# A decoder's last cross-attention on Trainium2: the keys' weights folded into the queries' weights, computed on the chip

## What is computed

```
x = x + attn(ln(x))                  layer 0, 16 heads, softmax
x = x + xattn(ln(x), ctx)            layer 0, 16 heads, softmax
x = x + ffn(ln(x))                   layer 0, int4 weights and a low-rank part
x = x + attn(ln(x))                  layer 1, 16 heads, rotary, sigmoid
x = x + xattn1(ln(x), ctx)           layer 1, one head: the change is here
x = x + experts(ln(x))               layer 1, two of 64 matrices per chunk of 128 rows

xattn1:  query = z @ Wq + bq;  key = ctx @ Wk + bk;  value = ctx @ Wv + bv
         weights = softmax(query @ key.T * 256 ** -0.5);  weights @ value
```

## Time and profile before

| | |
|---|---|
| median of 3 runs | 1092.56 us (1092.5 to 1093.98) |
| the profiled execution: its own time, its span | 1093.21 us, 1091.3 us |
| TensorE busy, matmuls / weight loads | 1026.3 us (94%) / 802.1 us (74%) |
| VectorE, ScalarE, GpSimd busy | 758.2, 637.0, 578.8 us |
| TensorE in the chain that ended last | 81% of the span |

### The profile page before, as it was taken

The page is one execution under the profiler, slowest core; times in us unless marked ns, Lnnn a source line. Parts: engine busy times, 40 slices in busy tenths (PEclk is TensorE's granted clock), DMA queues, the critical chain, the costliest instruction groups (busy, mean ns, idle before and its releaser), DMA issues.

```text
span 1091.3 us, 24379 instructions
## 1 busy us (share of the span) xinstructions
PE 1026.3 (94%) x8490; PEld 802.1 (74%) x8490; DVE 758.2 (69%) x1748; ACT 637.0 (58%) x1160; POOL 578.8 (53%) x924
## 2 busy tenths in 40 slices
PE   5689999999999999999999999999999999999976
PEld 4456777777766777777777778787878766888854
DVE  4577778788776656666677887777877643587772
ACT  2335666566566676666654566676767777555430
POOL 3343453554445545555557898787787720124340
PEclk9889999999999999999999999999999999999989
DMA  6976677656646445654453446767575892036556
GB/s 200 120 101 89 109 98 90 97 85 87 87 64 88 70 74 93 117 93 92 92 81 46 60 58 92 84 88 88 75 95 70 102 107 31 15 98 186 149 160 212
DMA packets 123626, 104.94 MB, mean 96 GB/s; under 512 B 26841, under 2 KB 123241, under 8 KB 123497
## 3 DMA queue, kind: packets, MB, share of 16 engines
q1 hardware_dynamic: 117794, 99.71, 56.9%
q10 hardware_dynamic: 5712, 3.68, 1.6%
HBM read 29.47 MB, written 4.19 MB: 31 GB/s over the span
## 4 chain that ended last, share of the span: by engine, by line
PE 81%; DVE 6%; DMA 4%; issue 3%; SPq 2%; ACT 2%; POOL 1%; ACTq 1%; POOLq 0%; DVEq 0%
PE l_sT L1096 11%; PE l_ring L1181 11%; PE l_o L1116 11%; PE l_copy L1162 8%; PE l_ring L1131 7%; PE l_ring L1218 7%; PE l_copy L1139 4%; PE l_ring L1201 4%; DVE l_nmax L948 3%; PE l_copy L1116 3%; PE l_ring L1229 3%; PE l_sT L1760 2%; DMA qstack<-l_qpart 2%; PE l_ring L1831 2%; SPq L506 2%
## 5 line engine op out<-in xcount | busy, mean ns | idle before, releaser
L948 DVE TENSOR_REDUCE l_nmax<-l_ring 128x2 f32<-128x512 f32 (+1 forms) x384 | 250.1, 676 | 105.3 <-PE l_ring L1131 99.7
L747 ACT ACTIVATE l_probs<-l_sT 128x1024 f32<-128x1024 f32 (+1 forms) x256 | 256.7, 1023 | 68.3 <-PE l_sT L1096 55.9
L1096 PE MATMUL l_sT<-qstack,kstack 99*128 99x256 bf16 (+2 forms) x1280 | 186.1, 272 | 0.5 <-ACT l_probs L747 0.5
L1131 PE MATMUL l_ring<-kstack,qstack 96*128 96x256 bf16 (+1 forms) x1024 | 140.1, 249 | 19.2 <-DVE l_nmax L948 6.1
L1096 PEld LDWEIGHTS l_sT<-qstack,kstack 99*128 99x128 bf16 (+2 forms) x1280 | 126.7, 104 | 20.8 <-issue 1.6
L1131 PEld LDWEIGHTS l_ring<-kstack,qstack 96*128 96x128 bf16 x1024 | 75.6, 98 | 75.7 <-DVE l_nmax L948 23.2
L1116 PE MATMUL l_o<-l_probs,v_heads 128*32 128x256 f32 (+1 forms) x2048 | 127.4, 383 | 0.0
L1181 PE MATMUL l_ring<-wT,l_zT 128*128 128x256 f32 x512 | 124.5, 381 | 1.0 <-DVE l_nmax L948 0.8
L606 POOL TENSOR_SCALAR factors<-mv 128x2 f32<-128x2 f32 (+1 forms) x77 | 21.7, 282 | 166.6 <-DVE mv L1005 140.5
L1162 PE MATMUL l_copy<-l_zT,wT 128*128 128x256 f32 x384 | 101.3, 396 | 3.6 <-ACT l_q L794 1.8
L1181 PEld LDWEIGHTS l_ring<-wT,l_zT 128*128 128x128 f32 x512 | 91.7, 190 | 13.5 <-issue 2.8
(11 more groups left out here) (207 smaller groups left out, 1972.6 us busy)
## 6 DMA issues: line engine op xcount, KB each, us to landing
qstack<-l_qpart SPq DMA_DIRECT2D x288, 128.0 KB, 4.4
kstack<-l_kpart SPq DMA_DIRECT2D x192, 128.0 KB, 5.6
kstack<-in_experts SPq DMA_DIRECT2D x36, 256.0 KB, 3.1
kstack<-l_kpart SPq DMA_DIRECT2D x96, 60.0 KB, 3.3
qstack<-in_experts SPq DMA_DIRECT2D x20, 256.0 KB, 3.1
out_y<-x_res SPq DMA_DIRECT2D x16, 256.0 KB, 3.7
l_cx<-in_ctx SPq DMA_DIRECT2D x32, 90.0 KB, 2.9
x_res<-in_x SPq DMA_DIRECT2D x1, 2048.0 KB, 15.8
```

What stands on the lines that cost most here:

```text
L747: act.activation(probs[buffer_of(g)][0:kp, :], sT[g % 2][0:kp, :], ACT.Sigmoid if sig(u) else ACT.Exp, scale=HD ** -0.5).then_inc(p_ok, 1)
L948: dve.tensor_reduce(nmax[u % 2][:, tt, h0:h0 + hb], bank("s", u, i)[:, 0:hb * sk].rearrange("p (h k) -> p h k", h=hb), AX_X, ALU.max, nega ...
L1096: i = pe.matmul(sT[g % 2][0:kp, j * S:(j + 1) * S], kstack[slot_of(u)][0:rows_used, col * width(u) + kt * kp:col * width(u) + (kt + 1) * k ...
L1131: m = pe.matmul(out[:, j * sk:(j + 1) * sk], qstack[slot_of(u)][0:STACK, (h0 + j) * S + tt * P:(h0 + j) * S + (tt + 1) * P], kstack[slot_o ...
```

## The change

Before, queries and keys are projected apart. After, scores are (z M + m) times the context itself: M is the queries' weights times the keys' weights transposed, m the queries' bias times the same. The context gets a column of ones, by which the keys' bias joins the product, so the context rows are 194 wide with a column of zeros. The values' bias is a row of the values' weights and meets the same column of ones. In detail:

- Four new jobs on the layers' copy bank, one each in periods 35 to 38, all behind `qT`: `ma` transposes the queries' weights, `mb` the keys' weights, `mc` multiplies them, `md` multiplies the queries' bias. TensorE fills the bank, ScalarE empties it; GpSimd clears the folded keys' buffer in `ma`.
- The jobs `k` leave TensorE and ScalarE, from DRAIN twice and from TAIL_ORDER. `s` reads the transposed context, of which three buffers are used instead of two.
- The eviction of the values goes from VectorE (an add of the bias) to ScalarE (a copy).
- In `t.w`, the values' bias is one row instead of a broadcast over 128 partitions, GpSimd clears one block of 128 partitions instead of two of 64, and SyncE waits for that before its last two loads.
- VectorE sets the ones and zeros columns of the context's two buffers once.

```diff
-        rows st e3 p1k vb rope_k fz sT4 p2q pa fxb e4 z e5 fst dk2 sT5 pb qT sT6 fa e6 ffac sT7 p2k kT dq1 xb e7 fac fb""",
+        rows st e3 p1k vb rope_k fz sT4 p2q pa fxb e4 z e5 fst dk2 sT5 pb qT ma mb mc md sT6 fa e6 ffac sT7 p2k kT dq1
+        xb e7 fac fb""",
...
-        "qB": (15,), "t.w": (20,)}
+        "qB": (15,), "t.w": (20,), "ma": (35,), "mb": (36,), "mc": (37,), "md": (38,)}
...
-TAIL_ORDER = "cl fac s q hash choose z y rows2 v pT rows k out mean add z2 cx"
+TAIL_ORDER = "cl fac s q hash choose z y rows2 v pT rows out mean add z2 cx"
...
+            def fold_pads():
+                pool.wait_ge(copy_full, copied["ma", 0, 0] + 1)
+                pool.memset(fold_k, 0.0).then_inc(fold_zeros, 1)
...
+            def folded_weights(job):
+
+                copy_out(job, 0)
+                halves = copy_bank[:, :].rearrange("p (k f) -> p k f", k=KT)
+                if job == "ma":
+                    act.wait_ge(ring_full, ring["pb", B - 1, 0] + 1)
+                    i = act.activation(fold_q, halves, ACT.Identity)
+                elif job == "mb":
+                    act.wait_ge(fold_zeros, 1)
+                    act.activation(fold_k[:, :, 0:P], halves[:, :, 0:P], ACT.Identity)
+                    act.activation(fold_k[:, :, P + LAST_C:2 * P - 2], halves[:, :, P:C], ACT.Identity)
+                    i = act.activation(fold_k[:, :, 2 * P - 2:2 * P - 1], t["col_c_bk"][:, :].unsqueeze(2), ACT.Identity)
+                elif job == "mc":
+                    i = act.activation(folded, halves, ACT.Identity)
+                else:
+                    i = act.activation(fold_col[:, :], copy_bank[:, 0:KT], ACT.Identity)
+                i.then_inc(copy_empty, 1)
...
+            def fold(job):
+                out = copy_slot(job, 0)
+                halves = out[:, :].rearrange("p (k f) -> p k f", k=KT)
+                if job in ("ma", "mb"):
+                    tail_weights_there(pe)
+                    for k in range(KT):
+                        for e in range(KT):
+                            i = pe.transpose(halves[:, k, e * P:(e + 1) * P], (raw_q if job == "ma" else raw_k)[:, e, k * P:(k + 1) * P],
+                                             ident[:, :])
+                elif job == "mc":
+                    pe.wait_ge(copy_empty, copied["mb", 0, 0] + 1)
+                    for e in range(KT):
+                        for k in range(KT):
+                            i = pe.matmul(halves[:, e, :], fold_q[:, k, e * P:(e + 1) * P], fold_k[:, k, :],
+                                          start=(k == 0), stop=(k == KT - 1))
+                else:
+                    pe.wait_ge(late_dma, LATE_DMAS)
+                    for e in range(KT):
+                        for k in range(KT):
+                            i = pe.matmul(out[:, e:e + 1], fold_k[:, k, e * P:(e + 1) * P], t["col_c_bq"][:, k:k + 1],
+                                          start=(k == 0), stop=(k == KT - 1))
+                i.then_inc(copy_full, 1)
...
-            for name in ("c_wq", "c_wk", "c_wv"):
+            for name in ("c_wq", "c_wk"):
                 sp.dma_start(w[name][:, 0, :], d[name][0:P, :]).then_inc(w_dma, 16)
                 rest = d[name].shape[0] - P
-                sp.dma_start(w[name][P - rest:P, 1, :], d[name][P:P + rest, :]).then_inc(w_dma, 16)
-            sp.dma_start(bc_v[:, :], d["c_bv"].rearrange("(a n) -> a n", a=1).broadcast_to((P, D))).then_inc(w_dma, 16)
+                sp.dma_start(w[name][0:rest, 1, :], d[name][P:P + rest, :]).then_inc(w_dma, 16)
+            sp.dma_start(w["c_wv"][:, 0, :], d["c_wv"][0:P, :]).then_inc(w_dma, 16)
+            sp.wait_ge(pads_ok, 1)
+            sp.dma_start(w["c_wv"][LAST_C:P - 2, 1, :], d["c_wv"][P:C, :]).then_inc(w_dma, 16)
+            sp.dma_start(w["c_wv"][P - 2:P - 1, 1, :], d["c_bv"].rearrange("(a n) -> a n", a=1)).then_inc(w_dma, 16)
...
-            for name in ("c_wk", "c_wv"):
-                pool.memset(w[name][0:2 * P - C, 1, :], 0.0).then_inc(pads_ok, 1)
+            pool.memset(w["c_wv"][:, 1, :], 0.0).then_inc(pads_ok, 1)
...
-        def keys(b):
-            act.wait_ge(ctx_ps, ctx_no("k", b) + 1)
-            if b < 2:
+        def values(b):
+            act.wait_ge(v_ps, v_no("v", b) + 1)
+            if b == 0:
                 wait(act, m["parts_free"])
...
+            if b > 1:
+                act.wait_ge(out_ps, b - 1)
+            act.activation(v[b % 2][:, :], v_bank[0:SC, 0:D], ACT.Identity).then_inc(v_out, 1)
...
-                    i = pe.matmul(s_bank[:, tt * SC:(tt + 1) * SC], qT[b % 2][:, k, tt * P:(tt + 1) * P], kT[b % 2][:, k, :],
+                    i = pe.matmul(s_bank[:, tt * SC:(tt + 1) * SC], qT[b % 2][:, k, tt * P:(tt + 1) * P], cxT[b % 3][:, k, :],
```

More of the change, by code:

```diff
@@ L211, in jobs_of @@
     return out
-TAIL_ORDER = "cl fac s q hash choose z y rows2 v pT rows k out mean add z2 cx"
-TAIL_LEAD = {"s": 0, "pT": 0, "out": 0, "q": 1, "k": 1, "v": 1, "z": 2, "rows": 3, "cx": 2, "cl": 3, "fac": -1, "add": -5, "y": -6}
+TAIL_ORDER = "cl fac s q hash choose z y rows2 v pT rows out mean add z2 cx"
+TAIL_LEAD = {"s": 0, "pT": 0, "out": 0, "q": 1, "v": 1, "z": 2, "rows": 3, "cx": 2, "cl": 3, "fac": -1, "add": -5, "y": -6}
 def tail_jobs(p):
@@ L285, in layers_stage @@
                 copies_before[u], last_outputs = len(copied), u
-            opens = job in ("z", "fz", "cx", "nT", "aT", "qT", "kT", "w", "qA") or job in ("qa", "ka") and kind_of(u) != "sigmoid"
+            opens = job in ("z", "fz", "cx", "nT", "aT", "qT", "kT", "w", "qA", "ma", "mb", "mc", "md") or job in ("qa", "ka") and kind_of(u) != "sigmoid"
             if opens:
@@ L313, in layers_stage @@
         attnT = sb("attnT", [P, KT, S], F32)
-        cx = [sb(f"cx{i}", [SC, C], F32) for i in range(2)]
+        cx = [sb(f"cx{i}", [SC, C + 2], F32) for i in range(2)]
         cxT = [sb(f"cxT{i}", [P, 2, SC], F32) for i in range(3)]
@@ L376, in layers_stage @@
             "ring_free": [(ring_empty, len(ring))]})
[L377 to L382, removed]
+        tail_weights_there = tail["weights_there"]
         def w_loads(eng, j, dst, done):
@@ L721, in _ @@
                         quantised(i)
+                    elif job == "ma":
+                        fold_pads()
                     elif job == "np":
@@ L847, in _ @@
                         lora_rows()
+                    elif job in ("ma", "mb", "mc", "md"):
+                        folded_weights(job)
                     elif job == "e":
@@ L1285, in _ @@
                         transposed_weight(u, raw[u % 4], copy_slot("w", u)).then_inc(copy_full, 1)
+                    elif job in ("ma", "mb", "mc", "md"):
+                        fold(job)
                     elif job == "qA":
@@ L1338, in tail_programs @@
     first_bank = [job for job in jobs if job[0] in ("z", "z2")]
-    second_bank = [job for job in jobs if job[0] in ("k", "cx")]
+    second_bank = [job for job in jobs if job[0] == "cx"]
     third_bank = [job for job in jobs if job[0] in ("v", "hash")]
@@ L1507, in queries @@
                 wait(act, m["whole_free"]["qk"[b]])
+                wait(act, m["fold_there"])
             else:
@@ L1557, in do @@
                 queries(b)
-            elif job == "k":
-                keys(b)
+            elif job == "v":
+                values(b)
             elif job == "cx":
@@ L1612, in rows2 @@
             normalise(z2, b).then_inc(rows2_ok, 1)
[L1614 to L1622, removed]
         def residual(b):
@@ L1679, in bits @@
                 dve.memset(work[:, 0, b:b + 1], float(2 ** b))
-                i = dve.memset(work[:, 1, b:b + 1], float(2 ** b - 2 ** NB))
-            link(i)
+                dve.memset(work[:, 1, b:b + 1], float(2 ** b - 2 ** NB))
+            wait(dve, m["cx_free"])
+            for buf in cx:
+                dve.memset(buf[:, C:C + 1], 1.0)
+                i = dve.memset(buf[:, C + 1:C + 2], 0.0)
+            i.then_inc(ones_ok, 1)
+            dve.wait_ge(ones_ok, 1)
         def do(job, b):
@@ L1759, in queries @@
                 for k in range(KT):
-                    i = pe.matmul(q_bank[:, j * S:(j + 1) * S], w["c_wq"][:, k, j * P:(j + 1) * P], zT[b % 2][:, k, :],
+                    i = pe.matmul(q_bank[:, j * S:(j + 1) * S], folded[:, k, j * P:(j + 1) * P], zT[b % 2][:, k, :],
                                   start=(k == 0), stop=(k == KT - 1))
             i.then_inc(q_ps, 1)
-        def keys(b):
-            weights_there(b)
-            pe.wait_ge(ctx_out, ctx_no("k", b))
-            for j in range(KT):
-                for k in range(KT):
-                    i = pe.matmul(ctx_bank[:, j * SC:(j + 1) * SC], w["c_wk"][:, k, j * P:(j + 1) * P], cxT[b % 2][:, k, :],
-                                  start=(k == 0), stop=(k == 1))
-            i.then_inc(ctx_ps, 1)
         def values(b):
-            weights_there(b)
-            pe.wait_ge(ctx_out, ctx_no("cx", b) + 1)
+            pe.wait_ge(ctx_out, b + 1)
             if b > 0:
```

(2 more changed lines are left out.)

63 lines of the change are left out of this document (33 added, 30 removed), and 14 rows, old and new, of the table DRAIN.

## The result

| | before | after |
|---|---|---|
| median of the runs | 1093.27 us (1092.5 to 1094.37) | 1105.07 us (1101.85 to 1108.33) |
| profiled execution, its span | 1093.21, 1091.3 us | 1106.16, 1104.3 us |
| granted clock over the span | 0.989 | 0.983 |

A forecast was written before the change was run, and what follows sets the result against it. TensorE was taken to bound the layers' sigmoid periods and the tail. Folds +7.2, SyncE's wait in period 20 +2.4 and tail -0.8 gave +8.8 us, 1101.4 us for the median, range 1097.2 to 1104.6.

The forecast's parts named there:

- The folds: Four sigmoid periods of the layers: waits plus work of ma, mb, mc, md cost +7.2 us (6.5 to 8.5).
- 0.93 for each wait: Behind the queries' transposes, TensorE waits 0.93 us per fold until ScalarE has emptied the shared PSUM bank.
- Rival 2: Layers: the four fold waits are absorbed, 3.7 of 7.2 us vanish, total +5.1, 1097.7 us; chance 10%.
- The tail: Removed keys jobs gain nothing in middle periods, as output waits for ScalarE's evictions; tail sum -0.8 us (-4.1 to +0.6).
- a bound (0.17): Tail's middle periods: if ScalarE overlapped both evictions, the output would start at 1003.33, gaining 0.17 us a period.
- about 0.5 was forecast for that far: Tail's start: removed keys job takes 0.89 off the first output, values' eviction adds 0.38 to the second; 0.5 left.
- t.w: Period 20: SyncE's wait for GpSimd's clearing delays the stack copies, so TensorE starts 2.4 us later (0 to 3.4).
- the same 4.2 to land: Period 20: after the twelfth stack copy at 469.47, an unchanged 4.2 us landing lets TensorE start at 473.7.
- rival 4: At 471.3 the long TensorE wait halves the clock, costing 2.5 us more: +11.3, 1103.9 us; chance 10%.
- a row of 2 us without work: Kernel's end, 1054 to 1056: clock stayed at 1.00 for the first 2 us without work, cited against the half clock.
- The forecast 3.0: At 471.3 TensorE stands 0.6 + 2.4 = 3.0 us waiting for the stack copies.

The follow-up runs named there:

- experiment 3: Changed kernel with the four folding jobs moved from the middle to the head of their periods; 1.0077 times the kernel before.
- experiment 1: Changed kernel with SyncE's wait for GpSimd's clearing and the two transfers behind it moved behind the stack copies; 1.0045 times the kernel before.
- experiment 6: Changed kernel with later SyncE wait, folds at period heads and tail order `z v pT rows2 y` (first kernel): 1.0004 times before; two other tail orders: 1.0002, 1.0005.
- experiment 2: Kernel before with only a SyncE wait for GpSimd's two clearings added ahead of the last of its seven loads; 1.0031 times before, +3.4 us.
- 4: Changed kernel with the tail's values and transposed-probabilities jobs put ahead of the experts' products; 1.0074 times the kernel before.
- 5: Changed kernel with the later SyncE wait and without the four folding jobs, so its output is not the reference's; 0.9993 times the kernel before.
- order `v pT z`: Changed kernel with later SyncE wait, folds at period heads and tail order `v pT z rows2 y`; 1.0002 times the kernel before.

## Why the prediction was right, and where it was not

**The folds: right, term by term.** Forecast 0.93 for each wait and 0.44, 0.44, 1.74, 0.89 of work, 7.23; measured 7.13 in the trace. Work by itself (experiment 3) 0.48, 0.48, 1.81, 0.98, which makes each wait 0.78 to 0.87. Rival 2, waits absorbed by the slack of the other engines, is out: the period after the four is 18.98 us, nothing was caught up, although TensorE's weight loads were busy 80% of it. Start-to-start times judged this rightly; the 80% read by the Trainium skill's page Perfetto Trace Analysis, section Identifying the Most-Contended Engine, would have promised room that the trace does not have.

**The tail: right in mechanism, near in size.** The output waits for ScalarE, and the middle periods gain nothing (8.43 to 8.39). Forecast was an output 1.01 behind pT, it is 0.91: ScalarE's second eviction begins 0.28 behind the first, 0.10 before the first's row ends, the overlap that I had as a bound (0.17). The first output came 0.8 us earlier (56.45 us behind the layers' last queries, 57.28 before), and first to second takes 6.48 instead of 6.20. Up to the last but one output the tail gained 1.2 (1.5 without folds), where about 0.5 was forecast for that far. The rest of the kernel gave it back in that profile: from there to the end 45.7 us before, 46.9 after, 45.9 in experiment 1, 47.6 in the first kernel of experiment 6. In the end part of the kernel before, TensorE waits 4.5 us for experts' weights and 7.3 us for VectorE; its scatter is as large as the tail's gain, so the forecast 0.8 of the tail is neither shown nor refuted.

**t.w: the term that was mis-sized.** Forecast +2.4 us, from "the same 4.2 to land" and TensorE's start at 473.7, with the half clock as a rival of 10%. The steps up to there hold: shifted by the 0.64 us that the changed kernel was ahead, the first copy goes out at 462.35 (forecast 462.43) and the twelfth at 469.58 (469.47). Two things then failed. First the landing: up to 5.6 us, not 4.2. While SyncE stood, the DMA engines ran empty, and then had the whole backlog at once; their share in 460 to 462 (last column but one), first of the kernel before:

```profile
460.00:462.00 2.00, 1.96 (x19) 1.75 (x17) 1.59 (x4) 1.69 (x5) 1.73 (x7) 1.00 0.78 183
```

And of the changed kernel:

```profile
460.00:462.00 2.00, 1.96 (x19) 1.76 (x17) 1.56 (x4) 1.66 (x5) 1.59 (x5) 1.00 0.02 6
```

The kstack copies landed in 4.7 to 5.7 us with the wait alone too (experiment 2), and in 2.8 to 3.3 with the copies ahead of the last weights (experiment 1). That the idle DMA engines behind a waiting queue are the cause was not tried by itself. Second, the clock: rival 4 happened, in each profile in which TensorE waited 3.9 us or more there (the changed kernel, experiments 2, 3 and 4), and in none in which it did not (before, 1, 5, 6). The Trainium skill, TensorE: Matmul & The Clock Gate, Part 1, says that idleness takes the array to half its clock; these traces agree, with 1.00 ahead of the wait and 0.50 behind it. In period 21 the changed kernel's profiled execution took 20.39 us instead of 14.44: 3.3 of the 5.95 are the longer wait, and the other 2.6 the groups at half clock, close to the 2.5 at which the rival was priced. Experiment 1 saves 5.3 us, of which 0.75 is its gain over the kernel before, so 4.6 for the term; experiment 2 has 3.4, the profiles 5.95 and 5.1. So the step that was mis-sized is the term of 2.4, where 3.4 to 6 were due. The total came near all the same, since the folds, two thirds of it, were right.

The 10% for the half clock was too little, and the trace of the kernel before could have said so. The prediction set a row of 2 us without work against a wait of 3.0, and said that no row shows a wait of this length amid full work. One nearly as long as the wait that came stands near the program's start, for the same kind of copy, on the timeline of the kernel before:

```profile
40.71 1.03 PE L1131 MATMUL l_ring<-kstack,qstack 96*128 96x256 bf16 x4 [3.99 <-DMA qstack<-l_qpart]
```

And busy by stretch, ahead of that wait and behind it:

```profile
34.72:36.72 2.00, 2.00 (x11) 1.44 (x9) 0.32 (x3) 1.68 (x3) 1.32 (x2) 1.00 1.17 117
40.71:42.71 2.00, 2.00 (x7) 1.62 (x8) 1.36 (x3) 0.00 (x0) 0.00 (x0) 0.50 1.21 114
```

TensorE was busy 2.00 of 2 us, waited 3.99 and came back at 0.50. A wait of 2.07 us up to 328.37 in the same trace left the clock at 1.00. The forecast 3.0 lies between the two.

## What to carry to other kernels

A wait put into a DMA queue is charged to whatever is queued behind it, and here it cost more than the delay: SyncE stood 2.2 us, the copies behind it landed in up to 5.6 us instead of 4.2, TensorE waited 3.9 us and came back at half clock. Before you price a new wait of TensorE, look in the whole trace for one of about its length and read the clock behind it. Put a transfer that needs another engine's work behind those that TensorE waits for, even if it is itself issued much later. A job taken out of an order is worth nothing if it covered another's eviction; reorder in the same step, so that something else does.

## What the runs showed that I had not expected

One wait amid full work was enough for the clock to fall: TensorE was busy 8.66 of 9 us up to 471, then stood for 3.9 us (4.1 in experiment 2). The granted clock was 1.00 until some 0.7 us before the end of the wait in the changed kernel, and to its end in experiment 2. It stayed at half for 6.8 us in one kernel and 3.4 in the other, with TensorE back at full work.

Shorter waits went either way. In experiment 6, at the same place of the program and behind 2 us of full work each, a wait of 2.24 us (up to 330.12, order `v pT z`) was followed by 1.00, and one of 2.31 us (up to 327.84, the first kernel) by 0.50; eight products behind it then took 3.15 us, 1.89 in the changed kernel. A wait of 2.19 us at 50 to 52 in experiment 1's kernel, where TensorE had been busy only in part (1.43 of 2 us just before it), was followed by 0.58 and 0.50. How long the wait is was thus not the only thing that decided it. What decides it in these cases stays open, and it is one source of the scatter between executions.
